# The second cross attention's query stage: GpSimd's weight remainder is moved ahead of its two additions

## What is computed

```python
q_hk  = (hidden_q @ Wq.T).reshape(B, S, H, K)               # "asking": H = 16 heads, K = 128
q_big = jnp.einsum('bshk,hkq->bshq', q_hk, w_kc_q)          # "widening": to 384
q_big = q_big * cos_q + rotate_half(q_big) * sin_q          # "turning": rotary positions
q_r   = jnp.einsum('bshq,hqr->bhsr', q_big, W_qr)           # "narrowing", together with W_kr:
k_r   = jnp.einsum('bld,hdr->bhlr', kv_r, W_kr)
scores = jnp.einsum('bhsr,bhlr->bhsl', q_r, k_r)
```

## Time and profile before

| | us |
|---|---|
| median of 3 runs | 2110.57 (2106.6 to 2114.03) |
| the profiled execution | 2113.88 |
| its span, first to last instruction | 2112.1 |
| TensorE busy | 1982.2 (94% of the span) |
| VectorE, ScalarE, GpSimd busy | 1202.1, 868.3, 1005.4 |
| the 32 units of the changed part | from about 845 to 1125 of the span |

### The profile page before, as it was taken

How to read it: one execution, slowest core, us unless ns; L and a number is a source line. 1 busy time by engine, 2 the same in 40 slices (tenths; PEclk the granted TensorE clock), 3 DMA queues, 4 the chain that set the end, 5 groups by cost and what they waited for, 6 DMA issues and landing times. The chain is left out here.

```text
span 2112.1 us, 29249 instructions
## 1 busy us (share of the span) xinstructions
PE 1982.2 (94%) x9274; PEld 1436.9 (68%) x9274; DVE 1202.1 (57%) x2691; ACT 868.3 (41%) x2163; POOL 1005.4 (48%) x928
## 2 busy tenths in 40 slices
PE   7989999999999999999997999989978999999996
PEld 6858998876688744666664899877755555555553
DVE  4577787467651022666656878769863343444444
ACT  3555555233312100344334555535514444454451
POOL 1257884212352100566667788475303444555552
PEclk9999999999999999999999999999988999999999
DMA  5552331200311100122134233210345999888886
GB/s 186 194 191 63 97 100 61 82 1 1 120 52 43 35 0 0 42 91 78 58 105 146 64 97 101 87 68 1 104 152 153 312 299 327 211 214 217 216 212 183
DMA packets 104948, 251.47 MB, mean 119 GB/s; under 512 B 14800, under 2 KB 40912, under 8 KB 96304
## 3 DMA queue, kind: packets, MB, share of 16 engines
q1 hardware_dynamic: 82224, 196.02, 27.5%
q0 software_dynamic: 21136, 51.11, 11.4%
q10 hardware_dynamic: 1440, 2.49, 0.3%
HBM read 279.44 MB, written 55.07 MB: 158 GB/s over the span
## 5 line engine op out<-in xcount | busy, mean ns | idle before, releaser
L99 PE MATMUL banks<-L1f_w,L1f_xT 128*128 x760 | 265.0, 492 | 1.8 <-issue 1.3
L2967 POOL DMA_INDIRECT moe_sums<-L1f_y,L1f_row x94 | 149.4, 1589 | 218.5 <-DVE L1f_is_who L2834 169.8
L99 PEld LDWEIGHTS banks<-L1f_w,L1f_xT 128*128 128x128 f32 x760 | 138.0, 192 | 81.6 <-issue 6.7
L160 POOL TENSOR_TENSOR rstd<-rstd,power 128x1 f32<-128x1 f32 x48 | 32.0, 667 | 221.4 <-DVE rstd L154 221.4
L2785 DVE SCALAR_TENSOR_TENSOR L1f_z<-banks,L1f_share,L1f_sg 128x192 f32<-128x192 f32 x95 | 39.7, 418 | 147.9 <-ACT L1f_sg L2718 146.9
L2975 POOL DMA_INDIRECT L1f_xg<-moe_rows,L1f_row x95 | 94.4, 993 | 61.5 <-DVE L1f_spare L2825 24.6
L2718 ACT ACTIVATE L1f_sg<-banks 128x192 f32<-128x192 f32 x95 | 31.4, 331 | 206.1 <-PE banks L99 143.3
L99 PE MATMUL banks<-L0f_down,L0f_z 128*128 128x512 f32 x256 | 111.1, 592 | 1.5 <-DVE L0f_z L2242 1.5
L99 PE MATMUL banks<-L0f_hT_hi,L0f_ug_hi 128*128 128x512 f32 x256 | 100.0, 391 | 0.0
L99 PE MATMUL banks<-L0f_hT_hi,L0f_ug_lo 128*128 128x512 f32 x256 | 99.6, 389 | 0.0
L99 PE MATMUL banks<-L0f_hT_lo,L0f_ug_hi 128*128 128x512 f32 x256 | 99.6, 389 | 0.0
(11 more groups left out here) (433 smaller groups left out, 5701.5 us busy)
## 6 DMA issues: line engine op xcount, KB each, us to landing
L1f_w<-in_experts SPq DMA_DIRECT2D x95, 1280.0 KB
L1f_laid<-moe_counts SPq DMA_DIRECT2D x59, 512.0 KB
w<-in_L1x_heads SPq DMA_DIRECT2D x16, 704.0 KB, 4.0
L0x_q<-L0x_far SPq DMA_DIRECT2D x20, 512.0 KB
L1x_q<-L1x_far SPq DMA_DIRECT2D x20, 512.0 KB
w<-in_L0x_heads SPq DMA_DIRECT2D x8, 1216.0 KB, 6.5
L0x_far<-L0x_away_far SPq DMA_DIRECT2D x8, 1024.0 KB
w<-in_wug SPq DMA_DIRECT2D x8, 1024.0 KB, 4.8
```

The lines of the kernel that those rows point to most:

```text
L99: ins = pe.e.matmul(out, w, m, start=first and n == 0, stop=last and n == len(pairs) - 1)
L160: pool.e.tensor_tensor(self.rstd[:, i:i + 1], self.rstd[:, i:i + 1], self.power[:, 0:1], ALU.pow).then_inc(self.rstd_set.sem, 1)
L2967: pool.e.indirect_dma_start(self.sums[j % 2][:, :], bass.IndirectOffsetOnAxis(ap=self.row[:, j:j + 1], axis=0), self.y[j % self.NY][:], No ...
```

## The change

In an odd unit, `wq_low` for head k // 2 + 2 is called behind the multiplication of `xn` by sines and ahead of the waits of the pair addition, no longer behind the rest addition. No instruction is added or removed; the order of four instructions on GpSimd changes in 14 of the 32 units from multiplication, pair addition, rest addition, remainder to multiplication, remainder, pair addition, rest addition.

```diff
@@ -1341,6 +1341,8 @@
             pool.wait_ge(self.swapped, 2 * k + 2)
             pool.e.tensor_tensor(self.by_tile(buf[:], 1), self.by_tile(buf[:], 1), self.table(self.sinq[:, 2:3], 1),
                                  ALU.mult).then_inc(self.rest_sin.sem, 1)
+            if k % 2 and k // 2 + 2 < XH:
+                self.wq_low(pool, k // 2 + 2)
             pool.wait_ge(self.sin_set, 2 * k + 2)
             pool.wait_ge(self.cos_set, 2 * k + 1)
             pool.e.tensor_tensor(y[:, 0:2], y[:, 0:2], self.turn_part[k % 2][:],
@@ -1348,8 +1350,6 @@
             pool.wait_ge(self.rest_sin, k + 1)
             pool.wait_ge(self.cos_set, 2 * k + 2)
             pool.e.tensor_tensor(y[:, 2], y[:, 2], buf[:], ALU.add).then_inc(self.rest_set.sem, 1)
-            if k % 2 and k // 2 + 2 < XH:
-                self.wq_low(pool, k // 2 + 2)
         self.first_keys(pool)
         self.pool_attention(pool)
```

## The result

The changed kernel takes 2094.33 us (median of 6 runs, 2091.59 to 2099.65) against 2109.78 before (6 runs). The ratio is 0.9931, 95% interval 0.9912 to 0.9951: 0.7% faster. The prediction was 2095.5 with a range of 2089 to 2104. The profiled execution took 2095.59 us.

What follows compares the result with a forecast made beforehand. TensorE was taken as the bound, standing still 14 times for GpSimd's remainder `ws_lo`. 0.77 + 13 x 1.10 = 15.1 us off the 2110.57 median, other parts costing nothing, gave 2095.5 us, range 2089 to 2104.

Steps and rivals of the forecast that it cites:

- 1.10 us, from starts: TensorE's ask waiting for GpSimd's remainder `ws_lo`: 1.10 us per wait between matmul starts, first 0.77, 15.1 us in all.
- The listed 11.5: Total of TensorE's 14 listed waits of the ask for `ws_lo`, 11.5 us, taken as the gain's lower bound.
- The additions moved back for nothing: GpSimd's pair and rest additions, made after the remainder, still end before unit 7's narrowing needs them: no cost.
- the cover: Distance from the pair addition's end to the narrowing that needs it, after the change: 3.7 us.
- The new wait for `ws_hi`: GpSimd's additions now stand behind a wait for ScalarE's weight split; margin 0.40 us, no loss; rival of late split 0.03.
- VectorE and GpSimd: Shared SBUF access: VectorE's remainder, held by the pair addition, ends 0.42 us behind it, just before the sines: no cost.
- The first rival: VectorE's remainder loses the shared port twice, the sines start 1.2 us late: gain only 9.2 us, 2101.4 us; chance 0.07.
- The clock rival: TensorE's low clock in the last units lasts longer and eats the gain: 2104 us or more; chance 0.04.
- the price without the cover: Without the distance before the narrowing, the additions moved back would cost TensorE up to the remainder's 1.27 us.

Runs made afterwards that it cites:

- Half the moves: Changed kernel with the remainder ahead of the additions in only 7 of the 14 odd units, behind them in the others: 2102.93 us, ratio 0.9964 to before.
- the second timing: The changed kernel as it is, timed again beside the run with unit 30 narrowed into the asks' bank: 2097.91 us, ratio 0.9936 to before.
- 3.4 us of added work: Changed kernel plus four unused GpSimd multiplications between remainder and pair addition in odd units 1 to 27: 2095.66 us, ratio 0.9930 to before.
- The run with two copies: Changed kernel with VectorE's weight remainder made twice in a row: 2104.45 us, ratio 0.9965 to before.
- the run with six: Changed kernel plus six unused GpSimd multiplications between remainder and pair addition in odd units: 2118.33 us, ratio 1.0035 to before.
- the run with eight: Changed kernel plus eight unused GpSimd multiplications between remainder and pair addition in odd units: 2161.77 us, ratio 1.0251 to before.
- the other bank: Changed kernel with unit 30 narrowed into the asks' bank: 2091.88 us, ratio 0.9905 to before; again 2092.59 us, ratio 0.9912.
- with the fold moved as well: Changed kernel with unit 30 narrowed into the asks' bank and the last fold ahead of unit 29's narrowing: 2093.41 us, ratio 0.9913 to before.

## Why the prediction was right

*The bound and the price of the wait.* The step "1.10 us, from starts" held: the part became 15.37 us shorter, with 15.1 forecast. The listed 11.5 would have been too small by a quarter. Half the moves gave half, so the sum is one over 14 nearly equal stalls. That the median came within 1.2 us of the forecast is in part luck: it fell by 15.5 us here and by 13.5 in the second timing (2111.38 to 2097.91). The shortening of the part does not have this scatter. What follows the units did start earlier with them, but in the profiled execution it then ran 3.2 us longer.

*The additions moved back for nothing.* Held, and the cover has the predicted size: 3.4 us of added work were free, 5.0 and 6.7 were not, and the difference is 3.7.

*The new wait for `ws_hi`.* Held: no gap ahead of the remainder in the profile after. How late a split would have to be was not tried.

*VectorE and GpSimd.* Held: the remainder ends behind the pair addition, by 0.41 us, and the sines start 0.26 before the last matmul of the widening (910.94 against 911.20), exactly as before (916.74 against 917.00). The first rival did not happen: VectorE won the turn. The run with two copies tried its price: 0.75 a pair was put on sines that start 1.5 us late; by the same distance to the widening's last matmul (916.15 and 915.04) they started 1.37 late, and it cost 0.66.

The Trainium skill, page "SBUF — State Buffer", section "SBUF: two separate sides", describes the access as an exclusive lock, which whichever instruction starts first has for its whole length. The runs agree: VectorE's remainder took 1.69, 2.61 or 1.53 us, each time to 0.41 or 0.42 behind the end of GpSimd's instruction. They agree on the order too, which the prediction left open as a turn that the page does not settle: VectorE's remainder started ahead of the rest addition (908.21 against 910.35, and 914.01 against 915.25 before) and went first, and the second copy started behind it and had to wait.

*The clock rival.* It did not eat the gain, but it is part of the scatter of this kernel. The narrowings of units 30 and 31 took 4.51 and 4.51 us before, 2.81 and 2.81 in the first profile of the change, 4.51 and 4.51 in the second, with the same idle times ahead of them (1.87 or 1.88, and 2.38). So the 3.4 us that the first profile gained there are not the change's.

*What the prediction had too simply* is the price without the cover, "up to the 1.27 us of the remainder". At about that size, a listed wait of 1.33 in the run with six, it was the wait and 0.25 us more, and the clock had no part in it. Carried on to the run with eight, the same reckoning failed: behind an idle time of 2.93 the clock's part came on top, and it cost 67 us where 31 were expected.

## What to carry to other kernels

Where one engine is busy nearly all the time, look at the wait that returns in its list, find the instruction that ends it, and ask what stands ahead of that instruction in its engine's order and how long those can wait; here two additions had 3.7 us to spare, and the one that was wanted stood last. Price a stall by the starts of the instructions around it, not by the listed idle time. Work that is moved back is free up to its slack, and from there each microsecond counts, or more than that where the clock falls too, so measure the slack as well as the wait.

## What was not expected of the hardware

A stall of TensorE cost about 0.25 us more than its listed idle time, in all sizes: 0.66 for 0.42, 1.10 for 0.85, 1.58 for 1.33. The rows show where it is hidden: the matmul ahead of the stall is listed with 0.39 us although the next could start after 0.23, which is 0.16, and behind the stall of the earlier trace rows the second matmul starts 0.31 and not 0.23 us after the first (918.24 and 918.55), which is 0.08.

An idle time of 1.33 us in each pair of 17.35 left the granted clock at 1.00; 2.93 in each pair of 20.5 was followed by 0.66 and by narrowings of 4.3 to 4.5 us in place of 2.73, fourteen times out of fourteen. In the tail, after 1.9 and 2.4 us, the same narrowings came out either way from one execution to the next. With the other bank, unit 31's took 4.51 after 2.86 us, and with the fold moved as well 2.81 after 2.83. So the length of the idle time just ahead does not decide it alone; what else does stays open.
